# Row maxima of a banded attention batch taken in two halves of eight heads, with four exponentials in the batch's first half

## Chip, cores and metric

One core of a Trainium2 chip runs the whole program. The metric is the device time of one execution in microseconds. Engines are named as in the profile: PE (TensorE), PEld (its weight loads), DVE (VectorE), ACT (ScalarE), POOL (GpSimd), SP (SyncE, which here issues every DMA).

## The reference, cut to what matters

```python
# x (16, 256, 512), ctx (16, 256, 512); 16 heads of 32, window 128
def xattn(q, k, v, wq, wk, wv, wo_w, wo_b):
    qp, kp = rope(q @ wq.T), rope(k @ wk.T)         # rope over the 512 columns
    vp = v @ wv.T
    scores = (q_h @ k_h.T) * sqrt(32)               # per head, keys at a distance of at most 128
    attn = softmax(scores)
    return (attn @ v_h) @ wo_w.T + wo_b
x = x + xattn(layernorm(x), ctx, ctx, wq, wk, wv, wo_w, wo_b)
x = x + ffn(layernorm(x))     # 512 -> 2048 -> 512; weights quantised to 8 bits, activations to 16
```

## The kernel before, in words

The program has three phases. Phase A treats the 16 batches of 256 tokens one after the other: layernorm, the three projections, the attention, the output projection and the residual, and beside them one sixteenth of the work on W_in. Phases B and C are the two feed-forward products; the change does not touch them. Phase A is a software pipeline: step b holds the attention of batch b, the projections of batch b+1, the output projection and residual of batch b-1 and the first layernorm's moments of batch b+2. Each engine has its own copy of `step(b, ...)` in its block, and `steps` runs it: steps 0 and 1 written out, steps 2 to 13 as six rounds of a hardware loop with two steps in each, steps 14 and 15 written out. So there are five jumps back, from an odd step to the next even one.

PE's part of a step has two halves. In the first it makes the scores of 16 heads (`scores`, L581, into a ring of two banks), and after each second head one of the tiles of the other batches: the two K tiles (`qk_tile`, L492 to L494), the transposes of the normalised x (`x_transposes`, L504, behind the wait for `ln1_norm`), `shares` (L514, which spreads the reciprocal denominators of batch b-1), the two Q tiles, and V in three pieces. A head's scores may overwrite a ring bank once DVE has taken the row maxima of the head two before (`max_done`). In the second half PE transposes the negated maxima (`max_transposes`, L590), ACT copies them into 32 rows of the stacked q for four heads (`max_copy`, L838), three DMAs on SP copy them on to the other twelve (`stack_max`, L349), and PE makes the transposed scores with the maximum already subtracted (`scores_t`, L612), one of 24 products of the output projection behind each (`o_products`, L565), and after each four heads a `clump` of products with V (L626) and with a one-hot matrix for the denominators (L639). ACT takes the exponential of each head (`softmax_exp`, L845) and POOL masks it (`band`, L1341). The list `third` says which PSUM bank each head's transposed scores use.

DVE's part: `row_maxima` of 16 heads (L1038, two instructions a head with an accumulator read each), and after pairs of them the list `between`: the reciprocal (`invert`, L1080), `ln2_moments` and `largest` of batch b-2's second half (L1000, L1002, L1020, L1024), `xt_rest` (L1071, the low part of the transposed x, for which the Q tiles wait), `rotate` of k (L1061 to L1064), `normalise` (L1085). Then `split_max` (L1043, L1045), `rotate` of q, `quantise_win` (L1091 to L1098), `ln1_moments(b + 2)` (L1000, L1002, L1012, L280, L281), and `residual` (L1031), `ln2_moments` and `largest` for batch b-1's first half, then `residual` of its second half. POOL turns the moments into scale and bias in 14 small dependent operations at the start of the next step (`ln1_scale`, L286 to L292, L1330, L1332), and ACT applies them (`norm1`, L801) before PE's `x_transposes`.

Of the kernel before, what the change touches and what calls it, by code (L numbers as in the profile page):

```python
# [86 lines left out]
def build(nc, t):  # L87
# [11 lines left out]
    with ExitStack() as ctx:  # L99
# [91 lines left out]
        third = [bank[i] for i in (0, 1, 3, 0, 1, 3, 0, 1, 0, 1, 4, 0, 1, 4, 0, 1)]  # L191
# [4 lines left out]
        den_bank = q_bank[1]  # L196

# [16 lines left out]
        max_stacked = [sem(f"max_stacked{i}") for i in range(1, NC4)]  # L214
# [29 lines left out]
        MAX_COPIES = 2  # L244
# [66 lines left out]
        def _(sp):  # L311
# [33 lines left out]
            def stack_max(b):  # L345

                sp.wait_ge(mT_done, MAX_COPIES * (b + 1))
                for i in range(1, NC4):
                    sp.dma_start(q_st[MROW:P, KC * i:KC * (i + 1)].bitcast(F32),  # L349
                                 q_st[MROW:P, 0:KC].bitcast(F32)).then_inc(max_stacked[i - 1], 16)  # L350
# [31 lines left out]
            def step(b, has_o, has_proj, has_xt, has_next):  # L382
# [4 lines left out]
                stack_max(b)  # L387
                if has_proj:
                    stack_group("k", b + 1, 0)
                    stack_group("k", b + 1, 1)  # L390
                    stack_group("q", b + 1, 0)
                    stack_group("q", b + 1, 1)
                    load_win(b + 1)
# [94 lines left out]
        def _(pe):  # L488
# [39 lines left out]
            def qk_tile(j, which, half):  # L528

                src = (t_hi, t_lo) if which == "q" else (cT_hi, cT_lo)  # L530
                if which == "k":
# [3 lines left out]
                    wait(pe, res_done, 2 * (j - 2) + half - 1)  # L535
                elif half == 0:
                    pe.wait_ge(xt_hi, 2 * j + 2)
                    pe.wait_ge(xt_lo, 2 * j + 2)
# [9 lines left out]
            def o_products(j, has_proj, after):  # L548

                for s in range(2):  # L550
                    if s == 1 and after is not None:
                        pe.wait_ge(exp_done, after)
# [18 lines left out]
            def scores(b, n):  # L571
# [4 lines left out]
                if n < 2:  # L576
                    wait(pe, exp_done, H * b)
# [7 lines left out]
            def max_transposes(b):  # L585

                pe.wait_ge(msplit, 2 * (b + 1))
                wait(pe, onorm, 2 * b)
                for qb in range(2):
                    mm = pe.transpose(pv_bank[1][:, qb * P:(qb + 1) * P], neg_max[:, qb], ident[:])  # L590
                mm.then_inc(mT_mm, 1)

            def scores_t(b, n, has_proj):

                if n in (0, 2):
                    pe.wait_ge(mT_done, MAX_COPIES * b + n // 2 + 1)
                elif n % KC == 0:
                    pe.wait_ge(max_stacked[n // KC - 1], 16 * (b + 1))
                if n < 2:
                    pe.wait_ge(max_done, 2 * H * (b + 1))  # L600
                elif n == 2 and has_proj:
                    pe.wait_ge(v_done, 2 * (b + 2))
                elif n == 2:
                    pe.wait_ge(res_done, 2 * (b - 1))
# [824 lines left out]
```

## Time and profile before

| | us |
|---|---|
| median of 3 runs (1310.17 to 1321.9) | 1314.15 |
| the profiled execution | 1319.03 |
| its span in the trace | 1316.1 |
| phase A, to the last clump of step 15 | 806.56 |
| steps 2 to 13 (from 146.00 to 719.15) | 573.15 |
| PE busy over the span | 1177.7 (89%) |
| DVE, ACT, POOL busy | 916.9, 636.5, 421.8 |

Times in the trace are from the start of the span. A step is counted from PE's first scores (L581) to the next step's. In the timeline a matmul's length overlaps the next one's start, so PE's work is read from the distances between starts; square brackets give the idle time before an instruction and what ended it. "issue" stands where the engine waited for nothing that the profile shows.

### The profile page before, as it was taken

To read this page: it belongs to the slowest core of one execution; us is meant where nothing else is said; L and a number is where in the kernel's file an instruction comes from. 1 tells how busy PE (TensorE), PEld (TensorE's weight loads), DVE (VectorE), ACT (ScalarE), POOL (GpSimd) and SP (SyncE) were. 2 spreads that over 40 slices of the span, in tenths; PEclk is the share of its full clock that TensorE was granted. 3 is DMA by queue.
4 is the path that set the end of the run, shared out by engine and by line. 5 is a ranking of instruction groups with operands and counts; after the bars stand their busy time and mean duration, and the time that the engine had idled before them with its cause. 6 is when DMAs were issued, how large, how long until landed. Compare 5 with 4: busy or idle time off the path is not lost.

```text
span 1316.1 us, 25753 instructions
## 1 busy us (share of the span) xinstructions
PE 1177.7 (89%) x7904; PEld 783.1 (59%) x7904; DVE 916.9 (70%) x2359; ACT 636.5 (48%) x998; POOL 421.8 (32%) x775
## 2 busy tenths in 40 slices
PE   2689998898998989999899877699999979999997
PEld 2568767777776776776776755345444434444443
DVE  4578768668667767866866862566666658888885
ACT  3243353354354354345335323455565547777774
POOL 2343464354445355345346423000000003111230
PEclk9899999999999999999999978899999999999999
DMA  7434553553463363364355261255555230467762
GB/s 240 113 84 115 163 125 93 145 143 82 134 154 93 112 180 75 113 172 105 100 156 132 53 176 45 80 187 204 185 184 199 72 129 8 145 223 226 249 211 88
DMA packets 91042, 180.82 MB, mean 137 GB/s; under 512 B 12880, under 2 KB 21328, under 8 KB 90960
## 3 DMA queue, kind: packets, MB, share of 16 engines
q1 hardware_dynamic: 90960, 179.92, 46.6%
q8 instruction: 28, 0.46, 0.1%
q14 instruction: 54, 0.44, 0.1%
HBM read 81.30 MB, written 41.94 MB: 94 GB/s over the span
## 4 chain that ended last, share of the span: by engine, by line
PE 50%; issue 26%; DVE 13%; ACT 6%; DMA 2%; POOL 1%; DVEq 0%; ACTq 0%; SPq 0%; POOLq 0%
PE bank L773 16%; PE bank L492 5%; PE bank L494 5%; PE bank L493 5%; PE bank L565 4%; PE bank L626 4%; DVE bank L1038 4%; PE bank L581 3%; PE bank L612 3%; PE bank L639 3%; ACT probs L845 2%; DMA q_st<-q_st 2%; DVE roped L1064 2%; DVE row_max L1038 1%; DVE rt L1062 1%
## 5 line engine op out<-in xcount | busy, mean ns | idle before, releaser
L1038 DVE CUSTOM_DVE_ANT_0 bank<-bank,mask 128x256 f32<-128x256 f32 x512 | 202.1, 457 | 95.6 <-PE bank L581 67.6
L773 PE MATMUL bank<-wout_int,g_hi 128*128 128x512 bf16 x512 | 195.8, 382 | 8.9 <-DVE g_lo L1283 8.8
L773 PE MATMUL bank<-wout_int,g_lo 128*128 128x512 bf16 x512 | 195.6, 382 | 0.0
L742 PE MATMUL bank<-qT_hi,win_int 128*128 128x512 bf16 x512 | 194.1, 379 | 1.4 <-DVE qT_lo L1201 1.4
L742 PE MATMUL bank<-qT_lo,win_int 128*128 128x512 bf16 x512 | 194.0, 379 | 0.0
L845 ACT ACTIVATE probs<-bank 128x512 f32<-128x512 f32 x256 | 139.0, 602 | 79.3 <-PE bank L612 79.0
L1341 POOL TENSOR_SCALAR_AFFINE_SELECT probs<-probs 128x256 f32<-128x256 f32 x256 | 109.3, 438 | 114.8 <-ACT probs L845 112.3
L1283 DVE TENSOR_TENSOR g_lo<-h_int,g_hi 128x512 f16<-128x512 f32 x128 | 104.0, 812 | 35.9 <-ACT g_hi L967 34.7
L612 PE MATMUL bank<-q_st,k_st 128*128 128x256 f32 x512 | 109.4, 299 | 14.3 <-DMA q_st<-q_st 6.4
L612 PEld LDWEIGHTS bank<-q_st,k_st 128*128 128x128 f32 x512 | 91.8, 192 | 48.5 <-issue 21.7
L581 PE MATMUL bank<-k_st,q_st 96*128 96x256 f32 x512 | 98.6, 307 | 20.8 <-DMA q_st<-q_lo 10.9
L940 ACT ACTIVATE h_ring<-bank,b_in,g_scale 128x512 f32<-128x512 f32 x96 | 73.5, 778 | 75.1 <-PE bank L742 57.7
L1225 DVE TENSOR_REDUCE hmax<-h_ring 128x512 f32 (+1 forms) x96 | 63.5, 683 | 60.4 <-ACT h_ring L940 58.3
L581 PEld LDWEIGHTS bank<-k_st,q_st 96*128 96x128 f32 x512 | 76.5, 194 | 39.2 <-issue 21.0
L1394 POOL TENSOR_TENSOR xq<-xq,b_out 128x512 f32<-128x512 f32 x32 | 49.3, 1569 | 154.2 <-DMA xq<-x_scratch 147.3
L791 ACT CAST k_hi<-roped 128x1024 fp32r<-128x1024 f32 x16 | 16.8, 1048 | 169.0 <-DVE roped L1064 169.0
L967 ACT CAST g_hi<-h_int 128x512 f16<-128x512 f32 x128 | 78.8, 615 | 39.8 <-PE bank L773 32.8
L773 PEld LDWEIGHTS bank<-wout_int,g_hi 128*128 128x128 f16 x512 | 50.4, 99 | 71.5 <-issue 11.4
L1321 POOL TENSOR_TENSOR x_res<-x_res,wo_b 128x512 f32<-128x512 f32 x32 | 41.0, 1302 | 149.6 <-DMA x_res<-in_x 149.6
L492 PE MATMUL bank<-t_hi,wq_hi 128*128 128x256 f32 x256 | 72.7, 284 | 18.0 <-DVE t_lo L1071 18.0
L742 PEld LDWEIGHTS bank<-qT_hi,win_int 128*128 128x128 bf16 x512 | 50.1, 98 | 62.4 <-DVE qT_lo L1201 3.3
L773 PEld LDWEIGHTS bank<-wout_int,g_lo 128*128 128x128 f16 x512 | 50.4, 98 | 61.1 <-issue 1.7
(145 smaller groups left out, 2762.4 us busy)
## 6 DMA issues: line engine op xcount, KB each, us to landing
hidden_scratch<-h_ring SPq DMA_DIRECT2D x96, 256.0 KB, 2.0
h_ring<-hidden_scratch SPq DMA_DIRECT2D x96, 256.0 KB, 2.9
k_st<-k_hi SPq DMA_DIRECT2D x128, 128.0 KB, 2.9
q_st<-q_hi SPq DMA_DIRECT2D x128, 128.0 KB, 2.5
xq<-x_scratch SPq DMA_DIRECT2D x16, 1024.0 KB, 5.9
x_ln<-in_x SPq DMA_DIRECT2D x16, 512.0 KB, 4.3
ctx_raw<-in_ctxT SPq DMA_DIRECT2D x16, 512.0 KB, 4.6
k_st<-k_lo SPq DMA_DIRECT2D x64, 128.0 KB, 2.4
```

What stands on the lines that cost most here:

```text
L492: pe.matmul(out, l_hi, r_hi, start=first, stop=False)
L493: pe.matmul(out, l_hi, r_lo, start=False, stop=False)
L581: mm = pe.matmul(ring[n % 2][:, qb * S:(qb + 1) * S], q_st[0:MROW, n, qb * P:(qb + 1) * P], k_st[0:MROW, n], start=True, stop=True)
L612: mm = pe.matmul(third[n][:, kb * S:(kb + 1) * S], k_st[:, n, kb * P:(kb + 1) * P], q_st[:, n], start=True, stop=True)
L742: mm = pe.matmul(bank[f % 4][:], win_int[:, c, f * P:(f + 1) * P], part[:, par, c], start=c == 0 and part is qT_hi, stop=c == KC - 1 and p ...
L773: mm = pe.matmul(bank[4 * par + u][:], part[:, f % 4, u * P:(u + 1) * P], wout_int[:, f], start=f == 0 and part is g_hi, stop=f == FC - 1 ...
L845: act.activation(probs[:, n % SLOTS].rearrange("p k q -> p (k q)"), third[n][:], ACT.Exp, scale=SCORE_SCALE).then_inc(exp_done, 1)
L940: act.activation(dst, bank[f % 4][:], ACT.Gelu, bias=b_in[:, f:f + 1], scale=g_scale[:, f:f + 1]).then_inc(gelu_done, 1)
L967: act.copy(g_hi[:, f % 4], h_int[:, f % 4]).then_inc(ghi_done, 1)
L1038: dve.tensor_tensor_reduce(sc, sc, mask[:, (1 - qb) * P:(1 - qb) * P + S], 1.0, NEG, ALU.add, ALU.max, row_max[:, qb, n:n + 1]).then_inc(m ...
L1283: dve.tensor_tensor(g_lo[:, f % 4], h_int[:, f % 4], g_hi[:, f % 4], ALU.subtract).then_inc(glo_done, 1)
L1341: pool.affine_select(out=far, in_=far, compare_op=ALU.is_ge, fill=0.0, base=1 - P, pattern=[[0, 2], [1, P]], channel_multiplier=1).then_in ...
```

## The change

The row maxima are split after eight heads: a first `split_max` on DVE after head 7, a first transpose on PE behind the scores of heads 8 and 9, two copies of two heads each on ACT and one DMA for the other four; the same again after head 15. The transposed scores of heads 0 to 3 move into PE's first half, all on bank 7, and those of 4 and 5 stand right behind it. `third` is new. The first half of the output projection is issued between the scores of heads 4 to 9, the second half, which now waits for the last `max_copy`, between 11 and 15; the clumps stand after heads 9, 10 and after the last product. On DVE `xt_rest` comes one pair of heads earlier, `normalise` two pairs earlier; `ln2_moments` and `largest` of the second half move from the first half of the following step to the end of their own, and `ln1_moments` now stands behind them. On ACT `centre` of the second half moves likewise and `split_hi` of k goes behind the copies of the first maxima and of the attention output. SP issues W_in's load earlier; POOL's `ctx_lo` and the split of q come later.

DVE, end of step 1. Before: quantisation, then the moments of x_ln, then the residual pair, the last instruction being the second residual:

```order
L1098 COPY win_amax<-w_s 128x1
L1000 BN_STATS bn<-x_ln 128x6
L1002 BN_AGGR mv<-bn 128x2
L1000 BN_STATS bn<-x_ln 128x6
L1002 BN_AGGR mv<-bn 128x2
L1012 TENSOR_SCALAR veps<-mv 128x2
L280 TENSOR_SCALAR rstd<-veps 128x2
L281 TENSOR_SCALAR rstd<-rstd 128x2
L1031 TENSOR_TENSOR x_res<-bank,x_res 128x512
L1000 BN_STATS bn<-x_res 128x6
L1002 BN_AGGR mv<-bn 128x2
L1020 COPY ln_mv<-mv 128x2
```

The same place with the change, from the second residual (L1065) on:

```order
L1065 TENSOR_TENSOR x_res<-bank,x_res 128x512
L1034 BN_STATS bn<-x_res 128x6
L1036 BN_AGGR mv<-bn 128x2
L1054 COPY ln_mv<-mv 128x2
L1058 TENSOR_REDUCE dmax<-rt 128x1
L1034 BN_STATS bn<-x_ln 128x6
L1036 BN_AGGR mv<-bn 128x2
L1034 BN_STATS bn<-x_ln 128x6
L1036 BN_AGGR mv<-bn 128x2
L1046 TENSOR_SCALAR veps<-mv 128x2
L282 TENSOR_SCALAR rstd<-veps 128x2
L283 TENSOR_SCALAR rstd<-rstd 128x2
```

The moments of x_ln now stand behind the second residual, its moments and a `largest`; one more `largest` follows them and ends the step.

PE, step 1, between the two Q tiles. Before, heads 8 and 9 alone:

```order
L494 MATMUL bank<-t_hi,wq_lo 128x256
L581 MATMUL bank<-k_st,q_st 128x256 x4
L492 MATMUL bank<-t_hi,wq_hi 128x256
L493 MATMUL bank<-t_lo,wq_hi 128x256
L494 MATMUL bank<-t_hi,wq_lo 128x256
```

With the change the transposes of the first eight heads' maxima follow:

```order
L497 MATMUL bank<-t_hi,wq_lo 128x256
L586 MATMUL bank<-k_st,q_st 128x256 x4
L600 MATMUL bank<-ident,neg_max 128x128 x2
L495 MATMUL bank<-t_hi,wq_hi 128x256
L496 MATMUL bank<-t_lo,wq_hi 128x256
L497 MATMUL bank<-t_hi,wq_lo 128x256
```

The second Q tile now stands behind an instruction that waits for DVE's `split_max`.

The diff, cut to its core:

```diff
-        third = [bank[i] for i in (0, 1, 3, 0, 1, 3, 0, 1, 0, 1, 4, 0, 1, 4, 0, 1)]
+        third = [bank[i] for i in (7, 7, 7, 7, 0, 1, 7, 0, 1, 7, 0, 1, 2, 0, 1, 2)]
+        max_bank = [pv_bank[0], kv_bank[1]]
-        MAX_COPIES = 2
+        MAX_COPIES = 4
+        HALF = H // 2
...
+            def stack_max(b, half):
+                sp.wait_ge(mT_done, MAX_COPIES * b + 2 * half + 2)
+                near, far = (q_st[MROW:P, HALF * half + o:HALF * half + o + KC].bitcast(F32) for o in (0, KC))
+                sp.dma_start(far, near).then_inc(max_stacked[half], 16)
...
+            def max_transposes(b, half, has_proj):
+                pe.wait_ge(msplit, 4 * b + 2 * half + 2)
+                if half == 0:
+                    wait(pe, onorm, 2 * b)
+                elif has_proj:
+                    pe.wait_ge(v_done, 2 * (b + 2))
...
+            def scores_t(b, n, has_o):
+                half, m = divmod(n, HALF)
+                if m in (0, 2):
+                    pe.wait_ge(mT_done, MAX_COPIES * b + 2 * half + m // 2 + 1)
+                elif m == KC:
+                    pe.wait_ge(max_stacked[half], 16 * (b + 1))
...
+                tiles[4] += [lambda: max_transposes(b, 0, has_proj)]
...
+                tiles[5] += [lambda: scores_t(b, 0, has_o)]
...
+                tiles[6] += [lambda: scores_t(b, 1, has_o)]
...
+                tiles[6] += [lambda: scores_t(b, 2, has_o)]
...
+                tiles[7] += [lambda: scores_t(b, 3, has_o)]
...
+                scores_t(b, 4, has_o)
+                scores_t(b, 5, has_o)
+                some(2)
+                max_transposes(b, 1, has_proj)
...
+                scores_t(b, 9, has_o)
+                clump(b, par, 0, has_proj)
+                scores_t(b, 10, has_o)
+                clump(b, par, 1, has_proj)
+                for n in range(11, H):
+                    scores_t(b, n, has_o)
+                    some(2)
+                some(2)
+                clump(b, par, 2, has_proj)
                 w_transposes(b, has_proj)
+                clump(b, par, 3, has_proj)
...
             def step(b, par, has_c, has_o, has_proj, has_xt):   # ACT
                 if has_proj:
                     norm1(b + 1)
-                if has_c:
-                    centre(b - 2, 1)
...
+                max_copy(b, 0, 0)
+                max_copy(b, 0, 1)
                 if has_o:
                     ot_lead(b - 1, 0, has_proj)
                     ot_lead(b - 1, 1, has_proj)
                 if has_proj:
+                    split_hi("k", b + 1)
+                softmax_exp(b, 0)
...
                 if has_o:                                        # DVE
                     between[0] += [lambda: invert(b - 1)]
-                    between[5] += [lambda: normalise(b - 1, 0), lambda: normalise(b - 1, 1)]
-                if has_c:
-                    between[1] += [lambda: ln2_moments(b - 2, 1)]
-                    between[2] += [lambda: largest(b - 2, 1)]
+                if has_proj:
+                    between[1] += [lambda: xt_rest(b + 1, 0), lambda: xt_rest(b + 1, 1)]
+                    between[2] += [lambda: rotate(b + 1, "k", 0)]
+                if has_o:
+                    between[3] += [lambda: normalise(b - 1, 0), lambda: normalise(b - 1, 1)]
+                between[3] += [lambda: split_max(b, 0)]
...
+                split_max(b, 1)
                 if has_proj:
                     rotate(b + 1, "q", 0)
                     rotate(b + 1, "q", 1)
+                if has_o:
+                    residual(b - 1, 0)
+                    ln2_moments(b - 1, 0)
                 quantise_win(b)
+                if has_o:
+                    residual(b - 1, 1)
+                    ln2_moments(b - 1, 1)
+                    largest(b - 1, 0)
                 if has_xt:
                     ln1_moments(b + 2)
                 if has_o:
-                    residual(b - 1, 0)
-                    ln2_moments(b - 1, 0)
-                    largest(b - 1, 0)
-                    residual(b - 1, 1)
+                    largest(b - 1, 1)
```

## Rows read from the trace of the kernel before

**Rows 1.** Windows by step: us, busy (x instructions) of PE, PEld, DVE, ACT, POOL; PEclk, DMA
```profile
100.25:146.00 45.75, 42.93 (x363) 34.45 (x359) 33.73 (x103) 19.33 (x34) 22.70 (x47) 1.00 0.48 124
...
575.43:623.56 48.13, 44.49 (x362) 35.16 (x358) 34.66 (x107) 20.05 (x35) 22.88 (x46) 0.96 0.47 123
...
765.56:806.56 41.00, 33.21 (x234) 22.56 (x230) 23.86 (x89) 13.46 (x26) 11.49 (x20) 0.79 0.38 115
```

**Rows 2.** Timeline of PE, step 11 and the start of step 12
```profile
575.43 0.74 PE L581 MATMUL bank<-k_st,q_st 96*128 96x256 f32 x4
...
582.15 1.04 PE L504 MATMUL bank<-ident,x_ln 128*128 128x128 f32 x8
...
587.14 0.36 PE L492 MATMUL bank<-t_hi,wq_hi 128*128 128x256 f32 x1 [1.27 <-DVE t_lo L1071]
...
590.04 0.64 PE L581 MATMUL bank<-k_st,q_st 96*128 96x256 f32 x4
...
594.28 0.50 PE L492 MATMUL bank<-wv_hi,cT_hi 128*128 128x512 f32 x1 [0.29 <-DVE roped L1064]
...
603.27 0.50 PE L612 MATMUL bank<-q_st,k_st 128*128 128x256 f32 x2 [0.28 <-ACT q_st L838]
...
605.96 0.51 PE L612 MATMUL bank<-q_st,k_st 128*128 128x256 f32 x2 [0.55 <-DMA q_st<-q_st]
...
608.58 0.80 PE L565 MATMUL bank<-wo_hi,t_hi 128*128 128x512 f32 x1 [1.18 <-ACT probs L845]
...
619.03 0.39 PE L565 MATMUL bank<-wo_hi,t_lo 128*128 128x512 f32 x1
...
623.56 0.74 PE L581 MATMUL bank<-k_st,q_st 96*128 96x256 f32 x4
...
631.07 1.04 PE L504 MATMUL bank<-ident,x_ln 128*128 128x128 f32 x8
```

**Rows 3.** Windows: the stretch of step 11 with a lowered clock, columns as in rows 1
```profile
609.00:612.00 3.00, 3.00 (x21) 1.56 (x24) 2.46 (x6) 0.61 (x2) 3.00 (x6) 0.50 0.33 74
```

**Rows 4.** Timeline of DVE: the moments of x_ln and the first residual in step 11
```profile
608.68 0.69 DVE L1000 BATCH_NORM_STATS2 bn<-x_ln 128x6 f32<-128x512 f32 x1 [0.22 <-DVE win_amax L1098]
...
612.07 0.17 DVE L281 TENSOR_SCALAR rstd<-rstd 128x2 int32<-128x2 int32 x1
612.27 0.69 DVE L1031 TENSOR_TENSOR x_res<-bank,x_res 128x512 f32<-128x512 f32 x1
...
614.17 0.17 DVE L1020 COPY ln_mv<-mv 128x2 f32 x1
```

**Rows 5.** Lines L1012 and L280: ns least/median/most, first and last start
```profile
L1012 DVE TENSOR_SCALAR veps<-mv x16: 169/338/485, 6.6 to 706.6; 128x2 f32<-128x2 f32 x16
...
L280 DVE TENSOR_SCALAR rstd<-veps x16: 170/662/671, 6.8 to 707.0; 128x2 int32<-128x2 int32 x16
```

**Rows 6.** Timeline of POOL and ACT behind step 11: the layernorm's scale and its use
```profile
621.81 0.19 POOL L286 TENSOR_TENSOR nt_t<-rstd 128x2 f32<-128x2 f32 x1 [0.16 <-issue]
...
626.73 0.22 POOL L1332 TENSOR_SCALAR nmr<-nmr 128x2 f32<-128x2 f32 x1 [0.20 <-POOL nmr L1330]
...
626.98 1.52 ACT L801 ACTIVATE x_ln<-x_ln,nmr,rstd 128x512 f32<-128x512 f32 x2 [3.07 <-POOL nmr L1332]
```

**Rows 7.** Timeline of DVE: the jump back at 622, and step 13's start without one
```profile
621.39 0.68 DVE L1031 TENSOR_TENSOR x_res<-bank,x_res 128x512 f32<-128x512 f32 x1
626.21 0.43 DVE L1038 CUSTOM_DVE_ANT_0 bank<-bank,mask 128x256 f32<-128x256 f32 x1 [4.13 <-issue]
...
671.83 0.43 DVE L1038 CUSTOM_DVE_ANT_0 bank<-bank,mask 128x256 f32<-128x256 f32 x1 [2.18 <-PE bank L581]
```

**Rows 8.** Timeline of DVE, first half of step 11
```profile
588.40 0.69 DVE L1061 TENSOR_TENSOR rt<-bank,rope 128x512 f32<-128x512 f32 x1
...
596.00 1.28 DVE L1085 TENSOR_TENSOR oT<-oT,bank 128x512 f32<-128x512 f32 x2
...
601.57 0.20 DVE L1045 SCALAR_TENSOR_TENSOR neg_max<-row_max,neg_max 128x32 fp32r<-128x32 f32 x1
```

More of the change, by code:

```diff
@@ L535, in qk_tile @@
                     wait(pe, res_done, 2 * (j - 2) + half - 1)
+                    if half == 0:
+                        wait(pe, exp_done, H * (j - 1))
                 elif half == 0:
@@ L576, in scores @@
                 if n < 2:
-                    wait(pe, exp_done, H * b)
+                    wait(pe, exp_done, H * b - 2 + n)
                 else:
@@ L833, in centre, with max_copy @@
                 act.activation(rt[:, s].rearrange("p c t -> p (c t)"), x_res[:, s], ACT.Identity, bias=mv[:, 1, s, 0:1], scale=-1.0).then_inc(y2_done, 1)
-            def max_copy(b, i, c=slice(0, KC)):
-                act.wait_ge(mT_mm, b + 1)
-                act.copy(q_st[MROW:P, KC * i + c.start:KC * i + c.stop, :],
-                         pv_bank[1][MROW:P, 0:S].rearrange("p (o t) -> p o t", o=1).to_broadcast([P - MROW, c.stop - c.start, S])).then_inc(mT_done, 1)
+            def max_copy(b, half, pair):
+                act.wait_ge(mT_mm, 2 * b + half + 1)
+                first = HALF * half + 2 * pair
+                act.copy(q_st[MROW:P, first:first + 2, :],
+                         max_bank[half][MROW:P, 0:S].rearrange("p (o t) -> p o t", o=1).to_broadcast([P - MROW, 2, S])).then_inc(mT_done, 1)
             def softmax_exp(b, n):
@@ L1039, in row_maxima, with split_max @@
                                              row_max[:, qb, n:n + 1]).then_inc(max_done, 1)
-            def split_max(b):
-                dve.wait_ge(max_done, 2 * H * (b + 1))
-                dve.tensor_scalar(neg_max[:, :, MROW:MROW + H].bitcast(F32R), row_max[:], -1.0, None, ALU.mult).then_inc(msplit, 1)
-                dve.wait_ge(msplit, 2 * b + 1)
-                dve.scalar_tensor_tensor(out=neg_max[:, :, MROW + H:P].bitcast(F32R), in0=row_max[:], scalar=-1.0,
-                                         in1=neg_max[:, :, MROW:MROW + H], op0=ALU.mult, op1=ALU.subtract).then_inc(msplit, 1)
+            def split_max(b, half):
+                dve.wait_ge(max_done, 2 * (H * b + HALF * (half + 1)))
+                wait(dve, mT_mm, 2 * b + half)
+                heads = slice(HALF * half, HALF * (half + 1))
+                hi, lo = (neg_max[:, :, MROW + o + HALF * half:MROW + o + HALF * (half + 1)] for o in (0, H))
+                dve.tensor_scalar(hi.bitcast(F32R), row_max[:, :, heads], -1.0, None, ALU.mult).then_inc(msplit, 1)
+                dve.wait_ge(msplit, 4 * b + 2 * half + 1)
+                dve.scalar_tensor_tensor(out=lo.bitcast(F32R), in0=row_max[:, :, heads], scalar=-1.0,
+                                         in1=hi, op0=ALU.mult, op1=ALU.subtract).then_inc(msplit, 1)
             def rotate(j, which, half):
@@ L1149, in step @@
                 if has_o:
-                    residual(b - 1, 0)
-                    ln2_moments(b - 1, 0)
-                    largest(b - 1, 0)
-                    residual(b - 1, 1)
+                    largest(b - 1, 1)
             steps(dve, step)
-            ln2_moments(NB - 2, 1)
-            largest(NB - 2, 1)
             invert(NB - 1)
@@ L1363, in step @@
                     bias_x(b - 1)
+                    ot_rest(b - 1, 0)
+                    ot_rest(b - 1, 1)
                 if has_proj:
```

120 lines of the change are left out of this document (53 added, 67 removed).

## Prediction

> **What bounds the kernel now.** I read the windows by step first. PE is busy 42.9 to 44.5 us of each step, DVE 34.7 and ACT 20.1 of step 11's 48.13 [rows 1]: PE sets the pace of phase A, and what is to be won is only what PE waits. I then read PE's timeline through one step and kept its gaps [rows 2]: 1.27 us before the first Q tile for the low part of x, 0.29 before V, and in the second half 0.28 for ACT's copy of the maxima, 0.55 for the DMA that spreads them, 1.18 for an exponential, the fifth of the eight that must come before the output projection's second half. One wait more shows only as distance: 7.51 us from the first scores to the x transposes in step 12 (623.56 to 631.07), 6.72 in step 11 (575.43 to 582.15). Step 12 begins behind the loop's jump back, where DVE resumes 4.13 us after its last instruction (4.82 from that one's start) with nothing to wait for; without a jump the gap was 2.18 us and ended with PE's scores [rows 7]. So the jump costs PE 0.8 us today. Last, the clock: behind the 1.18 us gap PE's granted clock was 0.50, its level of 1.2 GHz, for some 3.4 us from 608.6 [rows 3]. By the windows one such stretch falls in each of the last four of the six loop rounds. Half speed for 3.4 us costs 1.7 at most; I take 1.1, since part of PE's time there is a gap or a wait.
>
> **Second half of a step, from the first Q tile to the last product.** Before: 587.14 to 619.42, 32.3 us, 31.2 without the low clock [rows 2]. What goes: the waits of 0.28, 0.55, 1.18 and 0.29. Around each I count 0.26 more, as the printed idle starts at the modelled end of the last matmul and the first one after a gap takes longer: 3.3 us. The maxima of heads 0 to 7 are now copied and spread some ten microseconds before head 4 needs them, and heads 0 to 5 have their transposed scores before the first product of the output projection.
>
> What comes is a wait in PE's first half. The second Q tile now stands behind the transposes of the first maxima. On DVE, counted from the first Q tile's start (that start follows head 5's maxima by 0.35): rotation of k 2.05 (three operations of 0.69, 0.68, 0.73, of which the first is shown), two heads at 4 x 0.38, two `normalise` 1.2, the first split 0.42 [rows 8]. That is -0.35 + 2.05 + 1.53 + 1.2 + 0.42 = 4.9. PE has finished the tile and the scores of heads 8 and 9 at 3.6 (590.04 is 2.90 behind 587.14, and head 9 must wait for head 7's maxima). So PE stands 1.4 us. Behind it queue the Q tile, `qk_mm` and so ACT's `ot_lead`, the split of k and the first exponential; that one starts at 10.2, ready 1.4 us before head 1 needs the bank. Other additions: a second pair of transposes 0.15, 0.3 for ACT's second `v_copy` before the second transposes (they use its bank), 0.2 before head 15 for the exponential of head 12 behind `oT_copy` and `ctx_hi`, and 0.26 around each of three waits, partly overlapping. Sum 2.3. If `normalise` and the split were hidden, the 1.4 would be zero; if DVE came a rotation later, 3.4. Net for this part: -1.0 us, from -2.4 to +1.0.
>
> **From the x transposes to the first Q tile.** Before 4.99. `xt_rest` now comes before heads 4 and 5, so the low part is there at 2.45 and the tile follows head 5's maxima: 2.45 + 0.92 + 0.77 + 0.34 = 4.5. Gain 0.5.
>
> **From the last product to the next x transposes.** Before 4.14 (two clumps and the W_in transposes) plus 6.72, or 7.51 behind a jump: 10.9 or 11.65 [rows 2]. Here I expect the loss. `ln1_moments` used to end at 612.24, seven microseconds before the last product [rows 2, 4]; now it follows that product. The chain, from the product's end: residual, moments and copy 612.27 to 614.34, 2.07, plus 0.05; `largest` 0.65; the moments of x_ln, 3.56 as traced, but with 0.40 and 0.66 in two operations on two numbers that have taken 0.17 [rows 4, 5]. POOL was at work beside them; now it is idle there, so 2.85. That is 5.6. Then POOL's 14 operations, 5.14 us, and ACT's normalisation, 1.55 [rows 6]: 12.4, and PE starts at 12.5 instead of 10.9. In a step without a jump: +1.6 - 0.5 - 1.0 = +0.1 us, nothing. With 3.56 for the moments it is +0.8.
>
> Behind a jump DVE decides. Its last instruction, one more `largest`, ends at 6.3; with the 4.13 of rows 7 the first maxima start at 10.4, the first and second heads are done at 11.2 and 12.0, the third and fourth scores wait for them, the second K tile runs 12.3 to 15.1 and the transposes start at 15.15 against 11.65: +3.5 - 0.5 - 1.0 = +2.0 us. Five such steps. This is the term I trust least. The row does not say when the new code begins to come, only that it came 4.13 us behind; were it hidden, the step would be as the others (+0.1, less today's 0.8).
>
> The Trainium skill, "Runtime: NRT & Kernel Launch", section "Instruction fetch mechanics", says that a taken branch to a page outside the two pages held forces a fetch before execution goes on. By that rule the 4.13 follows DVE's last instruction wherever that ends, as I count; a fetch that ran ahead would give the other sum, 10 us less in all. It speaks against this change, and it is why I give the hidden fetch a small chance. The trace agrees so far: DVE stalls at 622 after a step that ended early, with the scores ready, and not where no jump is.
>
> **The sum.** Steps 4, 6, 8, 10, 12: 5 x 2.0 = +10. Steps 2, 3, 5, 7, 9, 11, 13 and 14: 8 x 0.1 = +0.8. Step 1, where the moments are not yet late: -1.5, of 45.75 [rows 1]. Step 0 has no output projection, so its second half runs at the pace of 16 exponentials; four are now done before: -2.5. Step 15 has no projections: DVE sets its first half and loses `ln2_moments` and `largest` (2.0) there, and of the second half 21 us, four transposed scores and the waits go: -5.7 of 41.00. Then `invert` need not wait for the same two operations: -1.5. Clock: I allow one stretch of 1.1 in each of the last five rounds where four had one: +1.1. Phases B and C: 0. Together +0.7 us on the profiled execution's 1319.03 (span 1316.1 and 2.9 around it). That execution lay 4.9 above the median of 1314.15, so for the median I say 1315.
>
> **Rivals.** Slower, by the late chain and the clock: PE gains one standstill of 1.4 and one of 1.6 in each step and one of 3.3 behind a jump. In step 15, with waits of that size, the granted clock was 0.79 over 41 us [rows 1]. If each of 14 steps has a stretch of 3.4 us at the lower level and pays 1.7, that is 23.8 where I have 5.5, and with the moments at 3.56 another 5.6: 1315 + 18.3 + 5.6 = 1339. For it: the gap before rows 3's stretch was only 1.18. Against: gaps of 1.27 in all steps mostly leave the clock alone. Chance 0.27.
>
> Slower since the four exponentials don't move: ACT is in order, and they stand behind `ot_lead`, which waits for the second Q tile. If that comes 2 us later still, heads 1 to 3 each wait about 0.5 for one bank and its exponential: 14 x 1.5 = 21, 1336. Against: 1.4 us of slack by my count. Chance 0.06.
>
> Faster: the code comes while DVE is still in its chain (-10), and the clock stays up (-5.5): 1300. For it: a total of 3.4 us of waits goes in each step, and the last step is sure to gain. Chance 0.25. My own case, gain and loss balancing, has 0.42: 1315 within 1%.
>
> **Numbers.** About 1% is what a measurement of this kernel tells from no change: 1301 to 1327. Range: the bounds of the jump (-10, +4 with 4.9 instead of 4.13 each), of the first split's wait (-20, +28 over 14 steps) and of the clock overlap in part; 1291 to 1342 leaves out about two in ten. Faster 0.26, same 0.42, slower 0.32.
>
> **What would show it.** Right: the profile after has PE waiting about 1.4 us for neg_max between the Q tiles and about 1.6 us for x_ln before the x transposes (12.5 from the last product); no wait for the DMA of the maxima; behind a jump DVE's first maxima 10 to 11 us after the last product and steps 2 us longer; step 15 about 35 us. Wrong: x_ln ready before PE asks; a DVE gap behind a jump of less than 2.5 us; first exponential later than V's first piece; more than one low-clock stretch a round.

## The result, and the profile after

The changed kernel takes 1353.54 us (median of four runs, 1352.72 to 1356.63), the kernel before 1315.36 beside it: ratio 1.031, 95% interval 1.027 to 1.034. It is slower by 3%; the prediction was 1315, its range ended at 1342. The profiled execution took 1356.63 us, span 1354.6.

Windows of the changed kernel by step: 1 (cut from 0.5 us before its start), 10, 11 and 12, and the first 41 us of step 15, columns as in [rows 1]:

```profile
102.75:147.83 45.08, 43.07 (x368) 34.62 (x364) 33.04 (x102) 21.37 (x37) 22.96 (x43) 1.00 0.44 118
548.87:604.01 55.14, 46.76 (x364) 37.74 (x360) 34.86 (x110) 21.35 (x36) 23.34 (x46) 0.91 0.40 105
604.01:651.07 47.06, 43.63 (x364) 34.71 (x360) 34.66 (x110) 21.36 (x36) 23.17 (x46) 1.00 0.47 123
651.07:706.78 55.71, 46.35 (x364) 37.35 (x360) 34.86 (x110) 21.35 (x36) 23.34 (x46) 0.91 0.39 105
803.02:844.02 41.00, 33.00 (x208) 23.68 (x208) 24.25 (x87) 13.68 (x25) 11.52 (x20) 0.75 0.45 129
```

There are two kinds of step here. Step 11, without a jump, is 47.06 us where it was 48.13 [rows 1]. Steps 10 and 12, behind a jump of DVE's loop, are 55.1 and 55.7. All five such steps (4, 6, 8, 10, 12) take 54.7 to 55.7, against 47.4 to 49.2 before: +35.6 us together, nearly the whole difference of the two profiles (37.6). What does a jump step do with 8 us more? DVE's timeline over the jump before step 10 (start, us, line, operation, tiles, and in brackets what it was idle for and why):

```profile
544.79 0.69 DVE L1065 TENSOR_TENSOR x_res<-bank,x_res 128x512 f32<-128x512 f32 x1 [3.85 <-PE bank L570]
...
551.00 0.69 DVE L1058 TENSOR_REDUCE dmax<-rt 128x512 f32 x1 [0.46 <-DVE rstd L283]
556.42 0.43 DVE L1072 CUSTOM_DVE_ANT_0 bank<-bank,mask 128x256 f32<-128x256 f32 x1 [4.73 <-issue]
...
559.01 0.08 DVE L1072 DVE_READ_ACCUMULATOR2_ANT row_max<- 128x1 f32 x1 [1.40 <-issue]
```

DVE stands 4.73 us between the last `largest` and the first row maxima, and 1.40 more in the middle of head 1; "issue" says that no semaphore held it. The five jumps show 4.99, 4.56, 4.64, 4.73, 4.70 and then 1.88, 1.60, 1.47, 1.40, 2.31. PE's timeline over the same jump, and one row of step 9, without one:

```profile
510.50 1.09 PE L507 MATMUL bank<-ident,x_ln 128*128 128x128 f32 x8 [1.27 <-ACT x_ln L828]
...
548.87 0.74 PE L586 MATMUL bank<-k_st,q_st 96*128 96x256 f32 x4
...
557.35 0.79 PE L586 MATMUL bank<-k_st,q_st 96*128 96x256 f32 x2 [4.91 <-DVE row_max L1072]
559.63 0.79 PE L586 MATMUL bank<-k_st,q_st 96*128 96x256 f32 x2 [1.49 <-DVE row_max L1072]
...
565.34 0.89 PE L507 MATMUL bank<-ident,x_ln 128*128 128x128 f32 x4
```

PE passes both stalls on. From the step's first scores to the x transposes it is 565.34 - 548.87 = 16.47 us; before it was 7.5 behind the jump of [rows 2], and in the changed kernel's steps without a jump it is 8.6 to 8.9. The second K tile, from 560.22, runs with 0.21 us from matmul to matmul where the first tile had 0.12. The windows of that stretch say why (third number from the end: the granted clock):

```profile
549.00:553.00 4.00, 3.43 (x28) 3.23 (x28) 1.83 (x6) 0.00 (x0) 1.17 (x6) 1.00 0.96 266
553.00:557.00 4.00, 0.00 (x0) 0.00 (x0) 0.58 (x3) 1.09 (x2) 1.58 (x8) 0.84 0.89 210
557.00:561.00 4.00, 2.17 (x8) 1.87 (x9) 2.60 (x7) 0.43 (x1) 0.00 (x0) 0.50 0.59 187
561.00:565.00 4.00, 4.00 (x21) 4.00 (x20) 1.71 (x9) 0.00 (x0) 0.44 (x1) 0.50 0.41 131
565.00:569.00 4.00, 3.87 (x23) 3.31 (x22) 2.12 (x7) 1.07 (x2) 2.07 (x2) 0.88 0.26 78
```

PE stands 4.9 us without a matmul, and the clock is at 0.50 (1.2 GHz) for about ten. The rows by group of PE's instructions add this up. The scores' line in the changed kernel, columns: busy, mean ns, idle time before it, and what ended that:

```profile
L586 PE MATMUL bank<-k_st,q_st 96*128 96x256 f32 x512 | 105.5, 315 | 62.9 <-DVE row_max L1072 49.9 <-DMA q_st<-q_lo 10.9
```

and in the kernel before:

```profile
L581 PE MATMUL bank<-k_st,q_st 96*128 96x256 f32 x512 | 98.6, 307 | 20.8 <-DMA q_st<-q_lo 10.9 <-DVE row_max L1038 9.8
```

PE waits 40 us more for row maxima, busy time aside.

### The profile page after: what moved, and what is told of

It reads as the page before. It is cut to its first block, busy times and chain, and to the rows that moved or that the text cites. A ratio compares the mean times of both kernels' runs of the same rounds, so it can differ in the third digit from the quotient of the medians.

```text
span 1354.6 us, 26066 instructions
## 1 busy us (share of the span) xinstructions
PE 1195.7 (88%) x7936; PEld 801.8 (59%) x7936; DVE 920.0 (68%) x2391; ACT 658.4 (49%) x1030; POOL 428.1 (32%) x775
## 4 chain that ended last, share of the span: by engine, by line
PE 47%; issue 29%; DVE 15%; ACT 5%; POOL 3%; DVEq 1%; DMA 1%; POOLq 0%; ACTq 0%; SPq 0%
PE bank L800 15%; PE bank L570 5%; PE bank L495 4%; PE bank L496 4%; PE bank L497 4%; PE bank L621 4%; PE bank L633 3%; DVE bank L1072 3%; PE bank L646 3%; PE bank L586 2%; DVE bn L1034 2%; DVE row_max L1072 1%; DVE roped L1101 1%; DVE oT L1122 1%; PE bank L600 1%
## 5 line engine op out<-in xcount | busy, mean ns | idle before, releaser
L873 ACT ACTIVATE probs<-bank 128x512 f32<-128x512 f32 x256 | 143.5, 605 | 88.4 <-PE bank L621 60.2
L586 PE MATMUL bank<-k_st,q_st 96*128 96x256 f32 x512 | 105.5, 315 | 62.9 <-DVE row_max L1072 49.9
L1380 POOL TENSOR_SCALAR_AFFINE_SELECT probs<-probs 128x256 f32<-128x256 f32 x256 | 114.5, 459 | 99.1 <-ACT probs L873 98.8
L621 PEld LDWEIGHTS bank<-q_st,k_st 128*128 128x128 f32 x512 | 87.6, 192 | 37.9 <-issue 14.8
L621 PE MATMUL bank<-q_st,k_st 128*128 128x256 f32 x512 | 104.5, 297 | 4.4 <-ACT probs L873 3.0
L866 ACT CAST q_st<-bank 32x512 fp32r<-32x512 f32 x64 | 34.0, 578 | 139.1 <-PE bank L600 138.8
L800 PEld LDWEIGHTS bank<-wout_int,g_hi 128*128 128x128 f16 x512 | 50.3, 98 | 72.4 <-issue 12.5
L769 PEld LDWEIGHTS bank<-qT_hi,win_int 128*128 128x128 bf16 x512 | 50.3, 98 | 62.2 <-DVE qT_lo L1240 2.5
L769 PEld LDWEIGHTS bank<-qT_lo,win_int 128*128 128x128 bf16 x512 | 50.4, 98 | 60.2 <-issue 1.1
```

The costliest lines, as they stand in the source:

```text
L586: mm = pe.matmul(ring[n % 2][:, qb * S:(qb + 1) * S], q_st[0:MROW, n, qb * P:(qb + 1) * P], k_st[0:MROW, n], start=True, stop=True)
L621: mm = pe.matmul(third[n][:, kb * S:(kb + 1) * S], k_st[:, n, kb * P:(kb + 1) * P], q_st[:, n], start=True, stop=True)
L769: mm = pe.matmul(bank[f % 4][:], win_int[:, c, f * P:(f + 1) * P], part[:, par, c], start=c == 0 and part is qT_hi, stop=c == KC - 1 and p ...
L800: mm = pe.matmul(bank[4 * par + u][:], part[:, f % 4, u * P:(u + 1) * P], wout_int[:, f], start=f == 0 and part is g_hi, stop=f == FC - 1 ...
L873: act.activation(probs[:, n % SLOTS].rearrange("p k q -> p (k q)"), third[n][:], ACT.Exp, scale=SCORE_SCALE).then_inc(exp_done, 1)
L1380: pool.affine_select(out=far, in_=far, compare_op=ALU.is_ge, fill=0.0, base=1 - P, pattern=[[0, 2], [1, P]], channel_multiplier=1).then_in ...
```

## The experiments

No kernel below leaves out any of the computation. Ratios are to the kernel before, timed beside it on the same chip.

**Is it the jump?** Theory: DVE's instructions behind the jump come late, and DVE now ends its step so late that nothing covers it. Three runs: the moments moved forward, the loop of DVE written out, the same for the kernel before; then the loop's code shifted.

```diff
 # moments_early, in DVE's step
+                if has_xt:
+                    ln1_moments(b + 2)
                 if has_o:
                     residual(b - 1, 1)
                     ln2_moments(b - 1, 1)
                     largest(b - 1, 0)
-                if has_xt:
-                    ln1_moments(b + 2)
-                if has_o:
                     largest(b - 1, 1)
 # dve_written_out
-            steps(dve, step)
+            step(0, 0, False, False, True, True)
+            step(1, 1, False, True, True, True)
+            for j in range(2, NB - 2):
+                step(j, j % 2, True, True, True, True)
...
```

> The changed kernel with one DVE block moved: ln1_moments(b + 2) stands before residual(b - 1, 1) again. Theory T (DVE's late end is the cause: it delays the normalised x in every step and moves the whole code fetch behind the jump into PE's path): DVE ends its step about 3.5 us earlier, non-jump steps go from 47.1 to about 45.3, jump steps from 55 to about 48.5, the time to 1306 (1298 to 1315). Rival R (the first split's wait and the new order on PE are the cause): no more than 1.5 us a step goes and the time stays above 1335.

Measured 1338.59 us, ratio 1.018 (1.015 to 1.021): 15 us gained where the theory had 47, and above the 1335 that I had given to the rival. The jump steps fell to 50.3 to 52.8 us, not to 48.5, and DVE still stood 3.5 to 3.7 and 2.2 to 3.7 us in them. The steps without a jump should have shrunk to 45.3 us and took 47.5 to 49.1. That needed an explanation of its own (below).

> The changed kernel with DVE's steps 2 to 13 written out instead of looped, the same instructions in the same order. Theory T: the stalls of 4.6 to 5.0 and 1.4 to 2.3 us and the low clock behind them go, jump steps fall from 55 to 47.2, the time to about 1315 (1310 to 1320). Rival F (code must be fetched anyway and stalls DVE wherever it ends late): more than 10 us of the 39 stay, 1325 or more.

Measured 1313.68 us, ratio 0.999 (0.997 to 1.001). Every step from 2 to 13 is now 46.9 to 47.3 us, and PE's idle time for row maxima is 12.4 us instead of 49.9. The same code without the jump is 39.9 us faster, and the instruction queue q14 moved 39 packets of 8 KB in the whole run where it had moved 59.

> The kernel before with DVE's steps 2 to 13 written out. Theory T: the jump costs it about 0.8 us in each of five steps and the first one up to 2, so 5 us go: 1310. Rival F: no difference, 1315.

Measured 1308.17 us, ratio 0.996 (0.993 to 0.999). In the kernel before the same jumps cost 7 us. So 33 of the 38 us are the jumps', and without them the changed kernel is 5.5 us behind.

> The changed kernel with 16 semaphore increments more on DVE before the loop, which move the loop's code by 16 instructions. Theory T2 (the second stall, inside head 1's maxima, is the next page of code, whose border lies ten instructions behind the jump's target): the 1.4 to 2.3 us stall goes from all five jump steps, with its share of half speed about 2.5 us each, and the time falls by 8 to 12, to 1343. Rival: the stall belongs to the instruction and not to its address; it stays and the time stays 1353.

The edit is sixteen extra semaphore increments ahead of DVE's loop. Measured 1340.44 us, ratio 1.021 (1.018 to 1.025). The second stall is gone from all five jumps, the first one is 3.5 to 4.8, and the steps are 50.7 to 51.9. The second stall hangs on where the loop's code lies.

**Which part of the change?** The halves without the moved normalisation, then the moved normalisation on the kernel before.

```diff
 # halves_alone, in DVE's step (and centre(b - 2, 1) behind norm1 on ACT)
                     between[0] += [lambda: invert(b - 1)]
+                if has_c:
+                    between[1] += [lambda: ln2_moments(b - 2, 1)]
+                    between[2] += [lambda: largest(b - 2, 1)]
...
+                quantise_win(b)
+                if has_xt:
+                    ln1_moments(b + 2)
                 if has_o:
                     residual(b - 1, 0)
                     ln2_moments(b - 1, 0)
-                quantise_win(b)
-                if has_o:
+                    largest(b - 1, 0)
                     residual(b - 1, 1)
-                    ln2_moments(b - 1, 1)
-                    largest(b - 1, 0)
-                if has_xt:
-                    ln1_moments(b + 2)
-                if has_o:
-                    largest(b - 1, 1)
```

> The changed kernel with the second normalisation put back where it was (second centring, moments and largest one batch later, DVE's step ends with the second residual sum). Theory (the loss comes from DVE's late end behind the jump, not from the halves): the jump steps lose their 16 us from the step's start to the x transposes and return to 7 to 9 us, total 1295 to 1315. Rival (the halves themselves lose, by the wait for neg_max between the Q tiles): 1330 or more.

> The kernel before with only the second normalisation moved into its batch. Theory (the late DVE end pays for the loss alone): every jump step shows a DVE stall of 4 to 5 us that PE waits out and a stretch at 1.2 GHz behind it, total 1340 to 1360. Rival (the two parts lose together only): 1325 or less.

Normalisation alone: 1346.54 us, ratio 1.022 (1.018 to 1.027). DVE ends 2.5 us behind the step's first scores and stalls 2.8 to 3.5 at each jump, less than the 4 to 5 expected; the jump steps take 51.0 to 52.2. The halves alone: 1337.99 us, ratio 1.016 (1.012 to 1.021), the rival's number, and not by the wait that the rival named. Their jump steps do go back to 6.7 us up to the x transposes, as DVE's first row maxima wait for PE and not for code. But a new wait stands in the second half. The halves alone, timeline of PE:

```profile
240.69 0.47 PE L621 MATMUL bank<-q_st,k_st 128*128 128x256 f32 x2 [1.75 <-DVE x_res L1066]
```

and of DVE:

```profile
236.22 0.69 DVE L1035 BATCH_NORM_STATS2 bn<-x_ln 128x6 f32<-128x512 f32 x1 [0.22 <-DVE win_amax L1136]
...
239.15 0.66 DVE L283 TENSOR_SCALAR rstd<-rstd 128x2 int32<-128x2 int32 x1
239.85 0.69 DVE L1066 TENSOR_TENSOR x_res<-bank,x_res 128x512 f32<-128x512 f32 x1
...
248.89 0.43 DVE L1073 CUSTOM_DVE_ANT_0 bank<-bank,mask 128x256 f32<-128x256 f32 x1 [3.96 <-PE bank L586]
```

Head 12's transposed scores use the bank that the first residual sum must have read first, and that sum stands behind the quantisation of W_in and the moments of x_ln. So the new table of banks is what needs the sum early, which the change's order of DVE gives it. I moved it there alone (e9), and with POOL's `bias_x` late (e10); what `bias_x` has to do with it comes first.

**The 48 us of steps without a jump.** In the run with the moments early (e1), the two operations of the first split of the maxima took 0.66 and 1.18 us in step 5, where the changed kernel has 0.35 and 0.17, and POOL's `bias_x` ran beside them. Two kernels, both with the moments early and DVE written out; the second also has:

```diff
                 if has_o:
-                    bias_x(b - 1)
                     ot_rest(b - 1, 0)
...
                 for n in range(H):
                     band(b, n)
+                    if n == 3 and has_o:
+                        bias_x(b - 1)
```

> Moments of x_ln before the second residual sum, and DVE's steps 2 to 13 written out, so no jump on DVE. Contention theory (POOL's bias_x, which now runs beside the first split of the maxima, makes its two small operations 0.66 and 1.18 us instead of 0.35 and 0.17, and PE waits 2.4 instead of 1.0 and falls to 1.2 GHz): steps of 48 us and more remain, total 1322 or more. Rival (the long steps were an aftermath of the jumps): steps of 45.3 to 46, total 1300 or less.

> As the run with moments early and DVE written out, with POOL's bias_x moved behind the band of head 3. Contention theory: the split's operations take 0.35 and 0.17 us again, first Q tile to the first transposes of maxima 5.0 us or less, steps of 45.3 us, total 1290 to 1300. Rival (DVE's own row of work sets that wait, whatever POOL does): as the other run within 0.5%.

Measured 1317.22 us, ratio 1.001 (0.999 to 1.004), and 1285.22 us, ratio 0.974 (0.969 to 0.979). One helper of POOL moved, 32 us. The first is under the 1322 that the contention theory gave, the second better than its 1290, and neither fits the rival. Step 2 without the move, timelines of DVE, POOL and PE:

```profile
160.61 1.01 DVE L1080 TENSOR_SCALAR neg_max<-row_max 128x16 fp32r<-128x16 f32 x1
161.66 1.18 DVE L1082 SCALAR_TENSOR_TENSOR neg_max<-row_max,neg_max 128x16 fp32r<-128x16 f32 x1
...
160.32 2.48 POOL L1364 TENSOR_TENSOR x_res<-x_res,wo_b 128x512 f32<-128x512 f32 x2 [11.41 <-DMA x_res<-in_x]
...
162.97 0.67 PE L600 MATMUL bank<-ident,neg_max 128*128 128x128 f32 x2 [2.87 <-DVE neg_max L1082]
```

and with the move, DVE and PE:

```profile
164.34 0.17 DVE L1080 TENSOR_SCALAR neg_max<-row_max 128x16 fp32r<-128x16 f32 x1
164.54 0.18 DVE L1082 SCALAR_TENSOR_TENSOR neg_max<-row_max,neg_max 128x16 fp32r<-128x16 f32 x1
...
164.86 0.43 PE L600 MATMUL bank<-ident,neg_max 128*128 128x128 f32 x2 [1.01 <-DVE neg_max L1082]
```

Its window of that step:

```profile
148.76:193.82 45.06, 43.13 (x365) 34.63 (x361) 36.31 (x109) 21.35 (x36) 23.30 (x47) 1.00 0.50 129
```

POOL's row holds two operations of 1.24 us each: 160.32 to 161.56 and on to 162.80. DVE's first small operation ends at 161.62 and its second at 162.84, each with one of POOL's. They are not slowed in proportion: each ends within 0.06 us of POOL's. The Trainium skill, "SBUF — State Buffer", section "Who interferes with whom", describes this: DVE and GpSimd share one pair of ports, which whoever starts first keeps for its whole instruction, against DVE's operations with two inputs in SBUF and some with one. By that rule each small operation waits for the POOL operation under way, and the trace agrees. PE's wait grew from 1.0 to 2.9 us (2.0 to 2.9 over the steps with a collision), and in nine of the twelve steps from 2 to 13 (47.5 to 49.2 us) the clock then fell (0.93 to 0.97 over the step); three (45.0) had short operations and escaped it. With `bias_x` late all twelve are 44.9 to 45.1.

> The halves alone, with the first residual sum and its moments put ahead of the quantisation of W_in, as in the changed kernel. Theory (the halves alone lost by head 12's wait of 1.75 us for that sum, which stood behind 7 us of other work of DVE, and by the low clock behind it; the jump itself is hidden, since DVE's step still ends with the second residual sum): the wait goes, 29.5 to 30.2 us from the first Q tile to the last product instead of 31.8 to 34.6, steps near 45.6, total 1285 to 1300. Rival (the halves lose elsewhere): 1320 or more.

> The same with POOL's bias_x behind the band of head 3. If bias_x already ends before the first split of the maxima here (it did in the run of the halves alone, whose split took 0.17 and 0.17 us), nothing changes: within 0.5% of the run beside it. If some steps still collide, 5 to 15 us less.

Measured 1333.34 us, ratio 1.013 (1.009 to 1.017), and 1313.93, ratio 0.998 (0.996 to 1.000). The wait for the sum is gone in both, but neither time is the 1285 to 1300 that I expected of e9, which has its rival's number. In e9 `bias_x` meets the split in all of steps 2 to 13 (in steps 4 to 7 the two operations take 1.03 and 1.19, 0.31 and 1.18, 0.81 and 1.19, 1.18 and 0.17). My expectation had taken the halves alone as free of it, and they were not (1.27 in step 2, 1.19 in step 4). Moving it brought 19 us, more than the 5 to 15.

The first gap at the jump is hidden in both: DVE ends 1.9 to 2.6 us ahead of the step's first scores, and its gap of 2.6 or 3.3 us ends with PE. In e10, which has the smaller lead, DVE then stands 1.2 to 1.5 us ("issue") at head 2 behind four of the five jumps, and the first Q tile starts 0.6 to 1.2 us late behind all five. The other 29 us between e10 and e8 have no run of their own; e10's trace has 26.3 us of PE waiting for row maxima against 12.3, and a stretch of low clock in ten of the twelve steps 2 to 13, where e8 has none.

**Why does one jump cost 1 us and another 8?** The best version with its loop back:

> The run of 1285 us with DVE's loop put back, so that only the jump is added. Theory (code loading behind the jump, uncovered where DVE ends late): the five steps at a jump are 50 to 53 us where the others are 45.0, total 1310 to 1325. Rival (the jump costs what it costs in the kernel before, 1.5 us a step): 1293 or less.

Measured 1335.31 us, ratio 1.015 (1.011 to 1.020): 50 us for five jumps, more than the 25 to 40 that I expected, though DVE ends 2.6 us earlier in the step than in the changed kernel. Its timeline of DVE at the jump before step 10, and the window of the stall:

```profile
539.93 0.43 DVE L1072 CUSTOM_DVE_ANT_0 bank<-bank,mask 128x256 f32<-128x256 f32 x1 [6.47 <-issue]
...
544.26 0.43 DVE L1072 CUSTOM_DVE_ANT_0 bank<-bank,mask 128x256 f32<-128x256 f32 x1 [3.08 <-issue]
```

```profile
533.46:539.93 6.47, 3.36 (x28) 3.15 (x27) 0.00 (x2) 1.52 (x2) 1.97 (x10) 1.00 0.96 251
```

So 4.7 us is no constant. The last but one number is the DMA engines' busy share, 0.96, and the DMA view shows instructions as transfers of their own. The changed kernel's stall, windows and DMA view (packets, MB, share):

```profile
551.69:556.42 4.73, 0.74 (x7) 0.54 (x5) 0.00 (x1) 0.51 (x1) 2.16 (x11) 0.92 0.94 224
```

```profile
q1 hardware_dynamic: 386, 1.05, 91.8%
q14 instruction: 2, 0.02, 2.0%
```

Code comes through the same DMA engines as data, and at a step's end SP issues up to twelve stacking DMAs of 128 KB and the load of the context, 512 KB. I held those back until DVE's first row maxima of the next step:

```diff
 # SP's step
                 if has_o:
+                    sp.wait_ge(max_done, 2 * H * b + 2)
+                    apart(sp)
+                    for n, i in (("k", 2), ("q", 2), ("k", 3), ("q", 3)):
+                        stack_group(n, b, i)
                     load_xres(b - 1)
...
+                    if has_o:
+                        load_ctx(b + 2)
                 stack_max(b, 0)
...
-                if has_next:
-                    load_ctx(b + 3)
-                if has_proj:
-                    stack_group("k", b + 1, 2)
...
```

> The run with moments early, bias late and the loop kept, with the stacking DMAs of heads 8 to 15 and the load of the context put behind DVE's first row maxima of the next step. Theory (the code packets stand in line behind these transfers): DVE resumes under 3.2 us behind its last instruction instead of 6.4 to 8.1, the second stall of 2.3 to 3.6 is under 1, jump steps 46 to 49 us instead of 54 to 57, total 1295 to 1310. Rival (the stall is the branch's own, whatever the traffic): 1328 or more.

> The run of 1285 us (moments early, bias late, DVE written out) with the same transfers held back. It has no jump on DVE: theory and rival both expect what holding back costs by itself, 1280 to 1292 if the stacked heads are still there in time, more only if head 8 or 12 waits for its DMA.

> The changed kernel (moments at the end of DVE's step, loop kept) with bias_x late and the transfers held back. Theory: the stall of 4.6 to 5.0 us behind the jump falls to 2.5 to 3.2 and the second one goes, PE keeps its clock in part: jump steps 49.5 to 52 instead of 55, total 1325 to 1340. Rival: as e15.

> The changed kernel with bias_x behind the band of head 3 and nothing else. In the changed kernel bias_x mostly misses the first split of the maxima (0.35 and 0.17 us), so by the contention theory little is to be had: 1340 to 1356. Rival (bias_x matters there too): under 1335.

| run | us | ratio (95%) | first stall | second | jump steps |
|---|---|---|---|---|---|
| e11, loop | 1335.31 | 1.015 (1.011 to 1.020) | 6.35 to 8.09 | 2.28 to 3.61 | 53.8 to 57.2 |
| e12, held back | 1312.83 | 0.997 (0.996 to 0.999) | 4.25 to 4.67 | 0.83 to 1.11 | 48.9 to 52.0 |
| e15, changed, bias late | 1350.66 | 1.026 (1.023 to 1.028) | 4.75 to 5.06 | 1.40 to 2.11 | 55.1 to 55.4 |
| e14, and held back | 1337.42 | 1.015 (1.012 to 1.018) | 3.01 to 3.23 | 0.88 to 1.10 | 51.9 to 52.1 |
| e13, no jump, held back | 1282.82 | 0.973 (0.971 to 0.976) | none | none | (45.0) |

Holding back costs nothing by itself (e13, beside 1285.22 of e8) and takes 22 and 13 us from the two kernels with the loop. The held-back run of the best version at the same jump, DVE and its windows, and then the window of e14's stall:

```profile
529.44 0.43 DVE L1071 CUSTOM_DVE_ANT_0 bank<-bank,mask 128x256 f32<-128x256 f32 x1 [4.41 <-issue]
...
531.55 0.43 DVE L1071 CUSTOM_DVE_ANT_0 bank<-bank,mask 128x256 f32<-128x256 f32 x1 [0.86 <-issue]
```

```profile
525.03:527.03 2.00, 2.00 (x18) 2.00 (x18) 0.00 (x0) 0.00 (x0) 1.06 (x6) 1.00 0.50 182
527.03:529.44 2.41, 1.35 (x12) 1.15 (x10) 0.00 (x1) 0.72 (x2) 0.90 (x5) 1.00 0.00 0
```

```profile
541.98:545.17 3.19, 0.75 (x7) 0.54 (x5) 0.00 (x0) 0.00 (x0) 1.56 (x8) 0.96 0.02 5
```

In e14's 3.19 us the DMA engines are as good as idle: that is the stall of this jump with nothing in the way. In e12 earlier transfers still fill the first part of the stall, and the last 2.4 us are without traffic. Holding back took 1.7 to 1.9 us from the first stall of the changed kernel with bias late and 2.0 to 3.4 from e11's. My expectations of e12 (under 3.2, 1295 to 1310 in all) were too low, and in e14 the second stall shrank and did not go; I had made the traffic's part too large. The greater part of the changed kernel's stall stays when the engines are idle.

Nor does a full share always make it long. The normalisation alone (e6), at its jump before step 10:

```profile
547.88:550.71 2.83, 1.08 (x10) 0.88 (x8) 0.00 (x0) 0.00 (x0) 1.43 (x8) 1.00 0.98 223
```

2.84 us with a share of 0.98, in code of another length. The rows of the instruction queue over the last two windows shown, e14's and then e6's, differ:

```profile
q14 instruction: 2, 0.02, 2.3%
```

```profile
q14 instruction: 1, 0.01, 1.0%
```

Before DVE goes on, the changed kernel, e1, e11, e12, e14 and e15 fetch two packets of code of 8 KB each (e1 and e11 three at step 4); the kernel before, the shifted loop (e4) and e6 fetch one. Taken packet by packet from the traces, DVE resumes 1.7 to 2.0 us after the last of these packets has landed, at each of the 45 jumps of the nine kernels whose gap ends in "issue". What varies is when the first one starts: within 0.1 us of DVE's last instruction in e14, 0.6 to 1.4 us behind it in the changed kernel, 2.6 to 2.8 at four of e11's five jumps. So the stall is a delay, which goes when the transfers are held back (e14), then one packet or two, and a rest of about 1.9 us. Why the delay is twice as long in e11 as in e15, at like shares, stays open.

**Is the best version's gain the change's?**

> The kernel before with DVE written out and bias_x behind the band of head 3. Its split of the maxima comes late in the step and takes 0.18 and 0.19 us in every step, so there is no collision to remove. Theory (the gain of the best versions comes from the halves): 1303 to 1313, as with DVE written out alone. Rival (bias_x costs the kernel before time elsewhere): 1295 or less.

Measured 1312.42 us, ratio 0.996 (0.994 to 0.998). The kernel before gains nothing from the move of `bias_x` (e3 without it: 0.996); so with the same two edits the changed order, its moments placed ahead of the second residual sum, is 27 us ahead, 2%. The change had a gain in it, and three things covered it: the jump, the place of the moments, and `bias_x`.

## Why the prediction was wrong, point by point

**Second half of a step: right.** PE waits 0.9 to 1.2 us for the first split (predicted 1.4), the DMA that spreads the maxima ends no wait of PE, and from the first Q tile to the end of the last product it is 29.7 us in the profile after, where I counted 30.2 (31.2 less 1.0). The gain is 1.5 against the kernel before's own steps at full clock, and 1.0 against its best steps with DVE written out (30.6): the right mechanism, and a little more than I said.

**From the x transposes to Q: right** (4.5 predicted and measured). **The late x_ln in steps without a jump: right.** PE waits 1.27 us for it, and the start of a step takes 8.7 us up to the transposes, 2.0 more than 6.72. The moments took 2.85 us, as counted. The rule "nothing gained, nothing lost" for those steps is borne out by steps 3 and 5, at full clock in both kernels (47.27 and 47.25 against 47.28 and 47.09); steps 11 (47.06) and 13 (47.05) are 1.0 shorter than 48.13 and 48.02, in which a stretch of low clock stood.

**"Behind a jump DVE decides ... +2.0 us. Five such steps": this is the term that failed.** The mechanism was the one that happened, DVE's stall behind its late end in PE's path; its size was +7.1 (35.6 over five, where the sum has 10). By its parts, start of the step to the transposes: predicted 10.95, measured 16.5. DVE's end came 0.7 us later than 6.3 behind the last product. The stall was 4.73 where I took over 4.13 from one row; the five of the kernel before are 3.9 to 4.9. The second stall, 1.4 to 2.3, I did not foresee at all; the trace before has one of 0.59 us, at head 3 of step 4, and I overlooked it. And 1.2 GHz for some ten microseconds costs 2.9 (second K tile and scores), where I had allowed 1.1 a round. PE stood still for 4.9 us in one piece, and I had taken the price of low clock from gaps of 1.2.

**Step 0, -2.5: wrong**, 47.84 against 45.62. **Step 15, -5.7: wrong**, about +1.7: its granted clock is 0.75 over 41 us, as low as before (0.79, [rows 1]), and the first output product starts 23.7 us into the step, 3.6 later than before, so the four transposed scores done ahead only moved in front of it. Neither was tried by itself. Step 0 varied from 45.2 to 48.8 us over kernels with the same code in it, and it goes with the granted clock there: 0.96 in e11 (45.17), 0.87 in the changed kernel (47.84), 0.83 in e9 (48.75). What sets that clock stays open. Step 14 lost 2.8 us (49.19 against 46.41), with a granted clock of 0.97; where the clock stays up (e2, e15) it has 46.4 and 46.5. Of the 37 us by which the profiled execution missed my sum, the jump steps hold 25.6, step 15 7.4 and step 0 4.7. That the same code without jumps comes to 1313.7, beside my 1315, is chance: my sum has 10 us for the jumps, and steps 0 and 15 are as far off there.

**The rivals.** The slower one, "by the late chain and the clock", had the right sign and 1339, but put the loss into 14 steps; it is in five, and the steps between them have the full clock. The one by the four exponentials did not come: in steps 2 to 13 no wait of PE over 0.1 us ends with an exponential. Of the faster rival's two conditions neither came. A hidden stall does exist (e5, e9), but only where DVE ends well ahead of PE's step.

**The rule of the Trainium skill.** The Trainium skill, "Runtime: NRT & Kernel Launch", section "Instruction fetch mechanics", says that a taken branch outside the two pages held forces a fetch before execution goes on. The runs agree with it: without the branch the stall is gone (e2), and code moved by sixteen instructions loses the second one (e4). It gives no price; here DVE stood 2.8 to 8.1 us.

## What to carry to other kernels

Before work is moved to the end of an engine's loop body, ask what covers that engine's jump: where DVE ended 2.6 us or more ahead of PE's step the jump was free (e5, e9), at 1.5 to 1.9 ahead it cost the first half 0.5 to 1.6 us (the kernel before, e10), and where DVE ended behind, the step grew by 3 to 12 us: the stall, longer while large transfers are under way, and then the pacing engine's clock after it has stood. Writing out only the loop of that engine removes it (39.9 us here). And where a small DVE operation stands on the critical path, look at what POOL does in that microsecond: an operation of 0.17 us took as long as the rest of POOL's 1.24.

## What the runs showed of the hardware that I had not expected

- The stall behind the jump of DVE's loop was 2.8 to 8.1 us over the kernels run; in the changed order with bias late it was 3.0 to 3.2 with the DMA engines idle and 4.8 to 5.1 with them full. It ended 1.7 to 2.0 us after the last packet of code had landed, however long it was. A second stall of 0.8 to 3.7 us (0.6 once in the kernel before) follows at head 1, 2 or 3, shrinks to about 1 when the transfers are held back, and goes in the changed kernel when the loop's code is shifted by sixteen instructions.
- After 4.9 us without a matmul PE had half its clock for about ten microseconds, though it was busy again for the last six of them.
- Operations of DVE on 16 numbers a partition took 1.01 and 1.18 us beside two additions of POOL, and 0.17 and 0.18 without them.
